# Another order for ScalarE's first norm and TensorE's turn of x, seven masked expert inputs instead of eight, and a reordered drain

## The reference, cut to what matters

```python
h = layernorm(x) * (1 + ca) + sa
x = x + ga * attn(h)              # wave positions, 33 taps a row, 8 heads, out_w, silu
h = layernorm(x) * (1 + cb) + sb
logits = h @ router_w.T + router_b
_, top = top_k(softmax(logits), 2)            # two of 8 experts for every row
mask = one_hot(top, 8).sum(-2)                # so the mask of a row sums to 2
out = einsum('bse,ehd,bsd->bsh', mask, expert_w, h) + einsum('bse,eh->bsh', mask, expert_b)
x = x + gb * out
```

## Time and profile before

| | us |
|---|---|
| median of 3 runs | 293.26 |
| the three runs | 293.26, 295.67, 291.19 |
| the profiled execution | 293.6 |
| its span, first to last instruction | 291.8 |
| TensorE matmul busy | 262.0 (90%) |
| VectorE busy | 262.0 (90%) |
| ScalarE busy | 226.9 (78%) |
| GpSimd busy | 62.7 (21%) |

### The profile page before, as it was taken

The page is one execution under the profiler, slowest core; times in us unless marked ns, Lnnn a source line. Parts: engine busy times, 40 slices in busy tenths (PEclk is TensorE's granted clock), DMA queues, the critical chain, the costliest instruction groups (busy, mean ns, idle before and its releaser), DMA issues.

```text
span 291.8 us, 5429 instructions
## 1 busy us (share of the span) xinstructions
PE 262.0 (90%) x1867; PEld 181.0 (62%) x1876; DVE 262.0 (90%) x543; ACT 226.9 (78%) x641; POOL 62.7 (21%) x59
## 2 busy tenths in 40 slices
PE   8899886899798999889998999889999989899995
PEld 3544642665486487647784569548884768476664
DVE  7989989998979999999999899989999999982671
ACT  4885899699897998699869989799779767655310
POOL 4103101800451023502080026202340300010100
PEclk9999999999999999999999999999999999999999
DMA  6560000020004000320014000500041004100101
GB/s 179 161 160 0 0 0 0 3 74 1 1 2 163 2 1 0 97 86 3 0 29 155 0 0 2 183 2 1 2 130 53 1 0 125 60 2 0 36 2 54
DMA packets 12011, 12.93 MB, mean 44 GB/s; under 512 B 1021, under 2 KB 10960, under 8 KB 11216
## 3 DMA queue, kind: packets, MB, share of 16 engines
q1 hardware_dynamic: 11540, 12.19, 13.9%
q10 hardware_dynamic: 444, 0.40, 0.5%
HBM read 10.44 MB, written 2.15 MB: 43 GB/s over the span
## 4 chain that ended last, share of the span: by engine, by line
ACT 31%; PE 26%; DVE 18%; POOL 12%; issue 11%; ACTq 0%; DVEq 0%; POOLq 0%
PE pE L1136 9%; ACT A L507 8%; DVE AT L835 8%; POOL rs L327 8%; ACT xn L405 4%; ACT c L490 4%; POOL nm L329 4%; PE pE L985 3%; ACT xn L371 3%; DVE T L802 3%; PE pY L1136 3%; PE pR L1028 2%; ACT hT L428 2%; ACT y L529 2%; DVE hm L902 2%
## 5 line engine op out<-in xcount | busy, mean ns | idle before, releaser
L802 DVE COPY_PREDICATED T<-mask,T 128x1472 f32<-128x1472 int16 (+9 forms) x54 | 76.2, 1411 | 0.5
L835 DVE TENSOR_TENSOR AT<-T,c 128x2064 f32<-128x2064 f32 x32 | 72.3, 2300 | 0.0
L1136 PE MATMUL pE<-hm,late 128*128 128x256 f32 x224 | 52.6, 386 | 0.0
L1136 PEld LDWEIGHTS pE<-hm,late 128*128 128x128 f32 x224 | 41.2, 190 | 6.6
L507 ACT ACTIVATE A<-pT 128x512 f32<-128x512 f32 x64 | 34.7, 600 | 12.6 <-PE pT L1051 12.5
L327 POOL TENSOR_TENSOR rs<-ve,mhalf 128x4 f32<-128x4 f32 (+1 forms) x18 | 32.5, 1806 | 44.3 <-DVE ve L715 37.5
L321 POOL TENSOR_SCALAR ve<-sq 128x4 f32<-128x4 f32 (+1 forms) x14 | 7.0, 502 | 162.9 <-ACT xn L371 162.9
L405 ACT ACTIVATE xn<-x,nm,rs 128x128 f32<-128x128 f32 x64 | 26.5, 485 | 16.1 <-POOL nm L329 16.1
L1051 PE MATMUL pT<-first,AT 128*128 128x128 f32 x256 | 34.2, 276 | 4.8 <-DVE AT L845 4.7
L1051 PEld LDWEIGHTS pT<-first,AT 128*128 128x128 f32 x256 | 28.3, 141 | 11.4 <-DVE AT L845 9.9
L507 ACT ACTIVATE A<-pR 128x512 f32<-128x512 f32 x64 | 35.2, 619 | 0.0
(11 more groups left out here) (145 smaller groups left out, 389.2 us busy)
## 6 DMA issues: line engine op xcount, KB each, us to landing
mkb<-mask_rows SPq DMA_DIRECT2D x6, 1024.0 KB, 5.3
x<-in_x SPq DMA_DIRECT2D x7, 256.0 KB, 6.1
out<-x SPq DMA_DIRECT2D x7, 256.0 KB, 5.3
late<-in_late SPq DMA_DIRECT2D x1, 592.0 KB, 3.9
mkb<-mask_rows SPq DMA_DIRECT2D x1, 512.0 KB, 3.6
x<-in_x SPq DMA_DIRECT2D x2, 128.0 KB, 3.7
wmod<-in_wmod ACTq DMA_DIRECT2D x1, 256.0 KB, 3.5
out<-x SPq DMA_DIRECT2D x2, 128.0 KB, 3.2
```

What stands on the lines that cost most here:

```text
L802: nc.vector.copy_predicated(rows[:, :, :, j0:j1], spread(mask[:, k, 0:w, j0:j1], [P, w, H, j1 - j0], 2), rows[:, :, :, j0 + (1 << bit):j1 ...
L835: nc.vector.tensor_tensor(cells_of(bt).rearrange("p h (j r) -> p h j r", r=BLK), spread(T[n % 2][:, bt, 0:H, 0:NB], [P, H, NB, BLK], 3), s ...
L1136: ins = mm(dst, weT[:, e, :], hm[b][:, e, :], start=False, stop=(e == E - 1))
```

## The change

Six edits:

1. ScalarE: `norm1` of unit i + 1 stands in passes i > 0 behind the second image's copies and in front of hT. It used to stand at the end of the pass before.
2. TensorE: `front_xT` stands behind both halves of turns and both halves of the second image's attention.
3. The last expert's weights are subtracted from the other seven and then doubled, once, by GpSimd (`expert_weights`, after `rstd1` of unit 2). As the mask of a row sums to 2, the expert sum is seven masked products with the differences and one plain product of h2T with the doubled weights. The mask rows, mkb, hm, `sel` and their transfers have seven rows instead of eight.
4. TensorE: `back_plain` replaces `back_biases`. Its plain product needs neither mask; the bias follows, and the wait for hm stands behind both.
5. Drain, VectorE: the residual and statistics of unit 7 stand before the last mask product of unit 6, and that product waits until GpSimd's power of unit 7 is done.
6. Drain, TensorE: two strings of warm-ups (5 and 6), and the experts of unit 6 dealt out in other pieces.

```diff
@@ GpSimd @@
+            def expert_weights():
+                pool.wait_ge(d_late, 32)
+                nc.gpsimd.tensor_tensor(weT[:, 0:EM, :], weT[:, 0:EM, :], spread(weT[:, EM, :], [P, EM, C], 1),
+                                        ALU.subtract).then_inc(g_we, 1)
+                pool.wait_ge(g_we, 1)
+                nc.gpsimd.tensor_scalar(weT[:, EM, :], weT[:, EM, :], 2.0, None, ALU.mult).then_inc(g_we, 1)
...
                 run(i, 2, rstd1)
+                if i == 0:
+                    expert_weights()
@@ ScalarE @@
                 second(i, -1, mid_A, 1)
+                if i > 0:
+                    run(i, 1, norm1)
                 run(i, 1, front_hT)
...
                 run(i, -1, back_mk)
-                run(i, 2, norm1)
+                if i < 0:
+                    run(i, 2, norm1)
@@ VectorE @@
-                                        spread(own, [P, E, L], 1), ALU.mult).then_inc(v_hm, 1)
+                                        spread(own, [P, EM, L], 1), ALU.mult).then_inc(v_hm, 1)
...
             set_ends(LAST, 0)
-            masked(LATE - 1, 1)
             residual(LATE)
             stats2(LATE)
+            dve.wait_ge(g_rs2, LATE + 1)
+            masked(LATE - 1, 1)
             route(LATE)
@@ TensorE @@
-            def back_biases(n, b, dst):
-                if n < LATE:
-                    pe.wait_ge(v_hm, before(n) + b + 1)
+            def back_plain(n, b, dst):
...
-                mm(dst, ebp[:, :], mkT_of(n)[:, b * L:(b + 1) * L], start=True, stop=False)
+                mm(dst, weT[:, EM, :], h2T_of(n)[:, b * L:(b + 1) * L], start=True, stop=False)
+                if b == 0:
+                    pe.wait_ge(a_mk, n + 1)
+                mm(dst, ebp[:, :], mkT_of(n)[:, b * L:(b + 1) * L], start=False, stop=False)
+                if n < LATE:
+                    pe.wait_ge(v_hm, before(n) + b + 1)
...
                 second(i, -1, mid_A, 1, 0)
-                run(i, 1, front_xT)
                 second(i, -1, mid_A, 1, 1)
                 second(i, -1, mid_attend, 1, 0)
                 second(i, -1, mid_attend, 1, 1)
+                run(i, 1, front_xT)
                 run(i, 1, front_row, 0)
...
             mid_attend(LATE, 1, 1)
+            warm_up(5, pT[0])
             mid_y(LATE)
-            back_experts(LATE - 1, 0)
+            warm_up(6, pT[0])
+            back_experts(LATE - 1, 0, range(0, 2))
             mid_gate(LATE)
+            back_experts(LATE - 1, 0, range(2, EM))
             mid_A(LAST, 0, 0)
...
             mid_attend(LAST, 0, 1)
-            back_experts(LATE - 1, 1, range(0, 3))
+            back_experts(LATE - 1, 1, range(0, 1))
             back_x2T(LATE)
-            back_experts(LATE - 1, 1, range(3, 4))
             mid_y(LAST)
+            back_experts(LATE - 1, 1, range(1, 3))
             back_logits(LATE)
             mid_gate(LAST)
-            back_experts(LATE - 1, 1, range(4, E))
+            back_experts(LATE - 1, 1, range(3, 6))
             back_mk(LATE)
+            back_experts(LATE - 1, 1, range(6, EM))
             back_mb(LATE, 0)
```

More of the change, by code:

```diff
@@ L20 @@
 E = 8
+EM = E - 1
 EPS = 1e-5
@@ L122, in build @@
         ebt = sb("ebt", [NP * E, 2, C], BF16); ebp = sb("ebp", [NP * E, C], BF16)
-        sel = sb("sel", [NP * E, E, P], BF16)
+        sel = sb("sel", [NP * E, EM, P], BF16)
         warm = sb("warm", [P, 512], BF16)
@@ L159, in build @@
         mkT = sb("mkT", [NP * E, BT * P], BF16); mkL = sb("mkL", [NP * E, L], BF16)
-        mkb = [sb(f"mkb{i}", [P, E, BT * P], BF16) for i in range(2)]
-        hm = [sb(f"hm{i}", [P, E, L]) for i in range(2)]
+        mkb = [sb(f"mkb{i}", [P, EM, BT * P], BF16) for i in range(2)]
+        hm = [sb(f"hm{i}", [P, EM, L]) for i in range(2)]
         moeT = sb("moeT", [P, BT * P])
-        scratch = nc.dram_tensor("mask_rows", (2, E, BT * P), BF16, kind="Internal").ap()
+        scratch = nc.dram_tensor("mask_rows", (2, EM, BT * P), BF16, kind="Internal").ap()
         pT = [bank("pT0"), bank("pT1")]
@@ L295, in masks @@
                     sp.wait_ge(d_mkb[n % 2], 16 * (n // 2))
-                sp.dma_start(scratch[n % 2][:, 0:w], mkT[0:E, 0:w]).then_inc(d_mk, 16)
+                sp.dma_start(scratch[n % 2][:, 0:w], mkT[0:EM, 0:w]).then_inc(d_mk, 16)
                 sp.wait_ge(d_mk, 16 * (n + 1))
@@ L895, in masked @@
                         dve.wait_ge(t_mb, 4 * late_image(n, b) + k + 1)
-                        nc.vector.tensor_tensor(hm[b][:, 2 * k:2 * k + 2, :],
-                                                four_banks(k)[:, :].rearrange("p (e l) -> p e l", e=2),
-                                                spread(own, [P, 2, L], 1), ALU.mult).then_inc(v_hm, 1)
+                        ne = min(2, EM - 2 * k)
+                        nc.vector.tensor_tensor(hm[b][:, 2 * k:2 * k + ne, :],
+                                                four_banks(k)[:, 0:ne * L].rearrange("p (e l) -> p e l", e=ne),
+                                                spread(own, [P, ne, L], 1), ALU.mult).then_inc(v_hm, 1)
                     return
@@ L1122, in back_mb @@
                         pe.wait_ge(v_hm, masked_before(before(n) + b - 1) + k + 1)
-                    for a in range(2):
+                    for a in range(min(2, EM - 2 * k)):
                         ins = mm(four_banks(k)[:, a * L:(a + 1) * L], sel[:, 2 * k + a, :], mkT_of(n)[:, b * L:(b + 1) * L],
@@ L1126, in back_mb, with back_experts @@
                     ins.then_inc(t_mb, 1)
-            def back_experts(n, b, own=range(E)):
+            def back_experts(n, b, own=range(EM)):
                 img = before(n) + b
@@ L1131, in back_experts @@
                 if own[0] == 0:
-                    back_biases(n, b, dst)
+                    back_plain(n, b, dst)
                 for e in own:
@@ L1135, in back_experts @@
                         pe.wait_ge(v_hm, masked_before(img) + e // 2 + 1)
-                    ins = mm(dst, weT[:, e, :], hm[b][:, e, :], start=False, stop=(e == E - 1))
-                if own[-1] == E - 1:
+                    ins = mm(dst, weT[:, e, :], hm[b][:, e, :], start=False, stop=(e == EM - 1))
+                if own[-1] == EM - 1:
                     ins.then_inc(t_moe, 1)
-            def back_biases(n, b, dst):
-                if n < LATE:
-                    pe.wait_ge(v_hm, before(n) + b + 1)
+            def back_plain(n, b, dst):
                 if b == 0:
-                    pe.wait_ge(a_mk, n + 1)
                     if n == 0:
                         pe.wait_ge(v_ebp, 8)
+                        pe.wait_ge(g_we, 2)
                     if n == LATE:
@@ L1224, in _ @@
             back_mb(LATE, 1)
-            back_experts(LATE, 0, range(6, E))
+            back_experts(LATE, 0, range(6, EM))
             back_experts(LATE, 1, range(0, 3))
@@ L1229, in _ @@
             back_mb(LAST, 0)
-            back_experts(LATE, 1, range(6, E))
+            back_experts(LATE, 1, range(6, EM))
             back_experts(LAST, 0, range(0, 4))
             back_out(LATE)
-            back_experts(LAST, 0, range(4, E))
+            back_experts(LAST, 0, range(4, EM))
             back_out(LAST)
```

6 lines of the change are left out of this document (3 added, 3 removed).

## The result

| | before | after |
|---|---|---|
| median of six runs each, us | 292.34 | 300.75 |
| lowest and highest | 290.19, 295.67 | 300.4, 301.92 |
| the profiled execution | 293.6 | 301.92 |
| its span | 291.8 | 300.1 |
| its mean granted clock | 0.998 | 0.983 |

The ratio is 1.030, with a 95% interval of 1.027 to 1.034: 3% slower. I had forecast 297.7 us with 291.0 to 300.5, and no measurable change as the likeliest verdict. The direction was right and the size was not: 4.4 us forecast, 8.3 us found in the profiled execution.

The account below looks back on a forecast made before the run. A closed chain of four legs, 31.77 us a pass, was taken as the bound. Shift 4.7 + drain 0.2 - 0.5 = 4.4 us gave 298.0 profiled, 297.7 median; own range 295.5 to 299.5, wider range 291.0 to 300.5.

Parts of the forecast that it names:

- four legs: Middle pass: a closed chain across TensorE, ScalarE and VectorE, 6.48 + 5.48 + 12.73 + 7.08 = 31.77 us, the whole pass.
- leg one: From TensorE's start on the second image's turns of AT to hT on ScalarE: 6.48 us, expected to become 6.96.
- Rival (a): VectorE's work alone sets a pass, so the order costs nothing and all 13 masks count: 289.2 us; chance 0.14.
- 4.60 + 1.50, less slack: Order's cost: 4.60 us up to the last full pass, 1.5 more in the one-image pass; residual 5.0 us later.
- Seven masked inputs: VectorE's 13 hm instructions each 0.28 us shorter at most; only two count, after the last residual wait: 0.56 us.
- I take the upper size and still no cost: GpSimd's subtract near 30 us: up to 4.5 us long, costing nothing; VectorE waits 0.96 us for ScalarE at 43.52.
- case (d): The subtract outlasts its cover at the start, or the drain loses more than summed: 2 us, 299.7; chance 0.07.
- rival (b): GpSimd's nm of the second norm is caught by VectorE's AT before lg: 6.4 us more, 304.1; chance 0.08.
- case (c): The gap of x's turn and the later drain let the granted clock fall: two us, 299.7; chance 0.05.
- leg four: From lg to VectorE's copy and TensorE's start on the second image's turns: 7.08 us, VectorE's own work.
- 4.7 + 0.9 less 5.0: Drain: shift on TensorE's side 4.7 us, last image's turns about 0.9 late from warm-ups, residual 5.0 later.
- The 0.5 us that I gave back before the mask's turn: Drain, TensorE: three experts instead of four stand before the mask's turn, taking 0.5 us off the sum.

Follow-up runs that it names:

- the early subtract: Kernel before with seven masks, squares ahead of the copies of the experts' sum, and GpSimd's subtract one pass earlier: 289.86 us, ratio 0.986.
- the subtract alone: Kernel before plus GpSimd's subtract and doubling, written into a tile nobody reads; weights, masks, order and drain unchanged: 294.14 us, ratio 1.001.
- TensorE's half: Kernel before with x turned behind the second image's attention on TensorE, ScalarE's order as before: 303.31 us, ratio 1.033.
- the order with the squares' swap: Kernel before with the new ScalarE and TensorE order, plus first-norm squares ahead of the copies of the experts' sum: 299.78 us, ratio 1.021.
- the squares' swap: Kernel before with ScalarE's squares for the first norm ahead of the copies of the experts' sum: 290.38 us, ratio 0.987.

## Why the prediction was too low, step by step

In short: two terms that the sum had at nothing failed, GpSimd's subtract (1.1 us) and the granted clock (2.3 us in the profiled execution); the legs, the order and the masks came as written, and the drain on the whole.

**The bound and its four legs: right.** Three kernels with leg one at 5.38, 6.48 and 7.03 us have passes of 30.69, 31.77 and 32.32 us: the pass moves by 1.63 where the leg moves by 1.65. Rival (a), VectorE's work alone, is out.

**The order: right in kind and size.** 4.60 + 1.50, less slack, gave 5.0 us up to the last full residual; alone on the chip it is 5.12. The new leg is 7.02 us where I had 6.96, and 6.32 in the last pass where I had 6.1.

**Seven masked inputs: right.** The group of the page that answers to the earlier trace rows (busy us, mean ns, idle us before and its releaser):

```profile
L918 DVE TENSOR_TENSOR hm<-mkb,h2T 128x1792 f32<-128x1792 bf16 x13 | 26.2, 2017 | 1.2 <-POOL rs L328 1.2
```

2017 ns instead of 2276, and in the middle passes the time saved turned into the wait before lg. The 1.2 us is the one in the drain, where the mask now stands behind GpSimd's power. Not foreseen: the cast that makes the selectors takes 1.07 us for 896 elements where it took 0.67 for 1024. That is 0.4 us more at 33 us. It costs nothing by itself: without the subtract the sums come 13.43 us behind `near` with seven rows (29.79 to 43.22) and 13.41 before, as the wait for ScalarE takes it in; beside the subtract that wait is used up and the 0.4 us count.

**GpSimd's subtract, "I take the upper size and still no cost": the first step that failed.** The cover that I named, the wait of 0.96 us, was there; what I set against it was GpSimd's next deadline instead of VectorE. The row shows VectorE's `near` held for the subtract's length. The cost is 1.93 us (2.27 - 0.34), with 0.40 for the cast, less 0.96 of cover and 0.27 by which the copies under a mask and what stands between them ran shorter (34.21 to 44.57, before 31.93 to 42.56): 1.1 us at the sums. I had this mechanism only as case (d), tied to the copies under a mask, with 0.07. Taking the subtract out of the changed kernel gives 1.4 us or more back at like clock; added to the kernel before, it does not show in the times at a full clock. The Trainium skill (GPSIMD Engine Reference, 3.1 Elementwise) gives the estimate of 2 us that the prediction states; by that page the duration agrees with the measured 2.09 us. Its section 8, Key points, names VectorE instructions with two SBUF inputs as those that contend, which I cited for rival (b) and did not apply here; the trace agrees: `near`, with two inputs in SBUF, takes 2.27 us against 0.34, and a reduction with one input beside the early subtract 0.47 us as without it.

**The clock, case (c), "0.05" and nothing in the sum: the second step that failed, and in the profiled execution the largest part of the miss.** In the profiled execution the pass from 58.59 to 93.54 is 34.95 us; the order alone, whose clock stayed at 1.00, has 32.62 there. The difference is 2.33 us: 1.24 from hT to the residual and 1.12 from there to lg, while leg one (7.03) and leg four are as in the others. In the median less is left of it: the changed kernel's run at 0.994 took 300.40 us, 1.5 less than the profiled one at 0.983. I had argued with TensorE's 29 us of 32 in a middle pass. The fall came in the earlier pass, where the first unit has only one image and TensorE was busy for 27.53 of 31.01 us before, and I had not looked at that stage's rows for it. Low clocks also appear in runs of the kernel before: 6 of its 45 later runs had 0.989 or less. In the same three sets the three kernels with seven masks and the subtract at its place, but not the new order, had it in 17 of 24 runs; the changed kernel had it in 5 of 6, the subtract alone in 4 of 10, the kernel with the early subtract in 0 of 4; of the orders without the masks, the order alone had it in 1 of 4, TensorE's half in 0 of 4, the order with the squares' swap in 3 of 4. So falls come more often with the seven masks and the subtract at that place; whether the order adds to it, and what brings a fall about, stays open.

**The drain: right on the whole, wrong in its parts.** From the last full residual to the last transposes I had -0.6 us; the shift goes from +8.75 (225.83 to 234.58) to +8.29 (288.67 to 296.96), that is -0.46. The warm-ups made TensorE less late at the last image's turns than I had: 0.18 us over the residual's shift (+8.93), where my terms give 0.6 (4.7 + 0.9 less 5.0). x2 is turned 7.16 us behind those turns, as written (7.1). The 0.5 us that I gave back before the mask's turn did not last, by the timeline of ScalarE and that of TensorE:

```profile
278.88 0.59 ACT L561 ACTIVATE mkT<-pL 24x512 bf16<-24x512 f32 x1 [3.25 <-PE pE L1154]
```

```profile
277.54 0.62 PE L1130 MATMUL pL<-ident,hit 128*24 128x128 bf16 x8
278.09 0.70 PE L1154 MATMUL pE<-hm,late 128*128 128x256 f32 x2
279.52 0.61 PE L1142 MATMUL pT<-mkT,sel 24*128 24x256 bf16 x4 [0.73 <-ACT mkT L561]
```

The mask's turn ends at 278.16, but the copy to mkT starts when the expert put behind the turn is through (278.79). The piece was moved behind the turn and its time came back as the copy's delay.

**Rival (b): not met.** GpSimd's nm before VectorE's AT ran at 145.42 for 0.58 us, 0.84 us ahead of AT at 146.26; it was not caught.

**The sum.** From `near` at 30 us to the last full residual the changed kernel needs 8.80 us more: 5.12 for the order, 1.1 for subtract and cast, 2.33 for the clock, 0.25 not attributed. Taking away the second and third from 301.92 us leaves 298.5, where the prediction had 298.0. Cases (c) and (d) had each been given 2 us and priced one at a time; they happened together, and a range that had let them add would have reached 301.7.

**What follows for the kernel.** The change works on the right leg in the wrong direction. What made leg one long was GpSimd's power caught beside AT, and the one swap that starts it 0.7 us earlier is worth 3.2 us (290.38 us against 293.56; ratio 0.987 [0.980, 0.993]). It beats both kernels with one line moved; with the seven masks and an early subtract the time is the same within the intervals (289.86 us).

## What to carry to other kernels

When the legs between four events sum to the pass, trust the sum: a microsecond in any leg is a microsecond in the pass, even on a VectorE that is 98% busy, and a saving outside the leg's own last arrival is only a new wait. A wait that a reorder removes must be weighed against everything that the reorder puts in the same leg; look first for what makes the awaited thing late. And small risks of different kinds (a VectorE instruction held at the start, a clock that falls in the stage with the pauses) do not exclude each other: price their sum too.

## What the runs showed of the hardware

- A GpSimd subtract of 128x896 took 2.09 to 2.22 us and held some VectorE instructions until it was over: a two-input one of 172 elements took 2.27 us instead of 0.34, a copy under a mask of 528 elements 2.14 instead of 0.80. A one-input reduction of 304 elements beside it took 0.47 us as without it.
- The reverse is as strong: a GpSimd operation of four elements beside VectorE's back-to-back AT instructions took 4.83 us (nm) or 6.00 us (the power) instead of 0.2 and 1.0 us, whichever of the two came to stand there. In the changed kernel the power took 5.98 us in some passes and 1.01 in another, with nobody waiting for it.
- The cast of the selectors took 1.07 us for 24x896 and 0.67 us for 24x1024, in every kernel with the one or the other. No run here shows why.
- The granted clock fell to 0.50 for some 3 to 10 us in ten of the fourteen profiled executions, in nine of them between 38 and 105 us and in one in the drain. In the profile of the kernel before it fell only at the very end; that it falls there too is taken from mean clocks down to 0.982. Ten more warm-ups in each of two passes moved the fall and did not end it.
- What a fall costs depends on where it lies and how long it lasts: 2.3 us for 10 us of half clock at 68 to 79 us in the changed kernel; nothing up to the sums for some 3 us of it at 40 to 44 us (the changed kernel with its order put back has them 14.54 us behind `near`, seven masks alone, with no fall before them, 14.56); some 1.1 us for 7 us of it with seven masks alone, and, as far as it is the fall that tells the runs apart, 1.5 us or more for some 3 us of half clock in the drain (the squares' swap, 291.94 against 289.99 to 290.43). A mean clock of 0.994 mostly cost nothing: 20 of 27 later runs of the kernel before at it took 293.2 to 293.5 us, those at 1.000 293.34 to 293.71.
